# Selective-scan block with a gated FFN: C multiplied in ahead of the transpose, and the sum over states kept in PSUM

## The reference, cut to what matters

```python
h = layernorm(x) * (1 + ca) + sa
dt, B, C = split(h @ x_proj_w.T, [128, 144])          # C: 2048 x 16
delta = softplus(dt @ dt_proj_w.T + dt_proj_b)
for t in tokens:                                       # state s: 256 x 16
    s = exp(delta[t] * A) * s + delta[t] * B[t] * h[t]
    y[t] = sum_n(s[:, n] * C[t, n]) + D * h[t]
x = x + ga * y
h = layernorm(x) * (1 + cb) + sb
x = x + gb * ((silu(h @ gate_w.T * gate_s) * (h @ up_w.T * up_s)) @ down_w.T * down_s)
```

## Time and profile before

| | |
|---|---|
| time, median of 3 (lowest to highest) | 377.23 us (377.08 to 378.97) |
| the profiled execution (span of its trace) | 381.0 us, 3907 instructions |
| first scan starts, last scan ends | 35.2 us, 339.6 us |
| DVE busy from 35.2 to 343 | 95% of it |

### The profile page before, as it was taken

The page is one execution under the profiler, slowest core; times in us unless marked ns, Lnnn a source line. Parts: engine busy times, 40 slices in busy tenths (PEclk is TensorE's granted clock), DMA queues, the critical chain, the costliest instruction groups (busy, mean ns, idle before and its releaser), DMA issues.

```text
span 381.0 us, 3907 instructions
## 1 busy us (share of the span) xinstructions
PE 260.1 (68%) x1212; PEld 197.4 (52%) x1212; DVE 316.1 (83%) x482; ACT 200.0 (52%) x320; POOL 207.9 (55%) x153
## 2 busy tenths in 40 slices
PE   8934544962652679756595897485779756669996
PEld 8534424552541556545374655373557545447774
DVE  2143999799999988999999899999998998993531
ACT  3431644571552686739535868386455556832610
POOL 2007464936597786465768665676685939321000
PEclk9995566775855569968997899779985968699999
DMA  5059940073040500620304216504022700000101
GB/s 171 3 151 369 235 67 0 3 163 60 19 92 1 110 2 0 174 51 20 92 2 73 37 55 137 89 0 112 1 63 48 158 10 0 0 2 0 55 2 58
DMA packets 15958, 25.57 MB, mean 67 GB/s; under 512 B 1344, under 2 KB 6656, under 8 KB 15936
## 3 DMA queue, kind: packets, MB, share of 16 engines
q1 hardware_dynamic: 15520, 24.48, 26.9%
q10 hardware_dynamic: 416, 0.81, 0.6%
HBM read 23.06 MB, written 2.23 MB: 66 GB/s over the span
## 4 chain that ended last, share of the span: by engine, by line
DVE 46%; PE 26%; issue 16%; ACT 6%; DMA 3%; POOL 1%; DVEq 0%; SPq 0%; ACTq 0%; POOLq 0%
DVE state L873 22%; DVE resid L796 11%; PE stateT L1056 5%; PE side L1003 4%; PE side L939 4%; PE side L1036 4%; DMA wmod_sb<-in_wmod 3%; PE side L1020 3%; DVE u L743 2%; DVE gates L771 2%; PE side L916 2%; PE stateT L900 1%; ACT decay L660 1%; DVE resid L708 1%; PE side L953 1%
## 5 line engine op out<-in xcount | busy, mean ns | idle before, releaser
L507 POOL TENSOR_TENSOR state<-u,brow 128x1024 f32<-128x1024 f32 x64 | 152.0, 2384 | 25.1 <-DMA brow<-bT_dram 25.0
L1056 PE MATMUL stateT<-ident,state 128*128 128x128 f32 x512 | 94.2, 336 | 102.1 <-DVE resid L796 68.2
L1056 PEld LDWEIGHTS stateT<-ident,state 128*128 128x128 f32 x512 | 72.7, 172 | 129.9 <-DVE state L873 116.3
L660 ACT ACTIVATE decay<-delta,A 128x512 f32<-128x512 f32 x128 | 87.0, 690 | 87.4 <-DVE state L873 85.0
L873 DVE TENSOR_TENSOR_SCAN state<-decay,last,state 128x512 f32<-128x512 f32 x96 | 117.4, 1264 | 9.2 <-ACT decay L660 9.1
L796 DVE SCALAR_TENSOR_TENSOR resid<-stateT,C_sb,resid 128x256 f32<-128x256 f32 x192 | 78.3, 469 | 0.0
L478 POOL COPY last<-state 128x2 f32<-128x2 f32 x48 | 10.0, 209 | 64.1 <-DVE state L873 63.8
L873 DVE TENSOR_TENSOR_SCAN state<-decay,state 128x512 f32<-128x512 f32 x32 | 37.1, 1202 | 2.8 <-ACT decay L660 2.8
L488 POOL TENSOR_TENSOR acc<-acc,prod 128x1024 f32<-128x1024 f32 x12 | 28.3, 2361 | 17.9 <-ACT prod L642 17.9
L1003 PE MATMUL side<-h_hi,ffn_hi 128*128 128x512 f32 x88 | 34.8, 479 | 0.6 <-DVE gates L771 0.6
L1003 PE MATMUL side<-h_lo,ffn_hi 128*128 128x512 f32 x88 | 30.8, 435 | 2.5 <-POOL h_lo L367 2.5
(11 more groups left out here) (98 smaller groups left out, 302.4 us busy)
## 6 DMA issues: line engine op xcount, KB each, us to landing
brow<-bT_dram SPq DMA_DIRECT2D x16, 1024.0 KB, 8.3
resid<-in_x SPq DMA_DIRECT2D x4, 512.0 KB, 11.1
out<-resid SPq DMA_DIRECT2D x8, 256.0 KB, 2.2
wmod_sb<-in_wmod ACTq DMA_DIRECT2D x1, 768.0 KB, 6.0
wmod_sb<-in_wmod SPq DMA_DIRECT2D x1, 768.0 KB, 11.6
ffn_sb<-in_gateT SPq DMA_DIRECT2D x1, 640.0 KB, 10.3
ffn_sb<-in_upT SPq DMA_DIRECT2D x1, 640.0 KB, 7.8
down_sb<-in_downT SPq DMA_DIRECT2D x1, 640.0 KB, 8.1
```

Of the source, the lines that this page charges most:

```text
L507: nc.gpsimd.tensor_tensor(state[j % RING_STATE][:, :, 0:S], u[:, c % 2, :, 0:S], b.unsqueeze(1).to_broadcast([P, HALVES, S]), ALU.mult).th ...
L660: nc.scalar.activation(decay[i % RING_DECAY][:, 0:S], delta[:, c % 2, h, 0:S], ACT.Exp, scale=A[:, h * N + n:h * N + n + 1]).then_inc(deca ...
L1056: ins = nc.tensor.transpose(to[:, b * D + h * P:b * D + (h + 1) * P], of[:, h, (2 * q + b) * P:(2 * q + b + 1) * P], ident[:, :])
```

## The change

- **C ahead of the transpose.** The scan no longer writes over its input: it reads `drv` (ring of 7) and writes `state` (ring of 4). Then state times C[n] goes back into `drv`, channel-major, in one 128x1024 instruction. DVE does this for states 0, 2, 4, 6, 8, 10, 12, 14, 15 (`times_c`), reading the row of C from the PSUM bank `rows_ps`. PE spreads that row there with a one-hot matmul on C split in two fp32r parts (`spread_row`). POOL does it for states 1, 3, 5, 7, 9, 11, 13 (`keep_c`), with rows of C that a DMA spreads over the partitions (`crow`).
- **Sum in PSUM.** PE's transposes of `drv` carry start=False and accumulate all 16 states, and the D term ahead of them, in the two banks `sums` (`add_state`, `add_dterm`). DVE adds `sums` to `resid` once a chunk (`x2`). `C_sb`, `acc2`, `prod` and the adds of L796 go.
- **Moved to POOL:** cap, u (now delta times `hmodg`, which ACT makes as a second copy of hmod scaled by ga), and nmr. Moved to ACT: the copy to `last`; in step 4 also h2 (from DVE), while lo of chunk 3 moves from DVE to POOL. POOL's drives run three slots ahead (`LEAD`).
- B and C are one product (`bc`), stored and read back together; `chi` (ACT) and `clo` (DVE) split C. Gates are single, and wmod lies in their memory. Side banks are three (six in step 4), placed by table. The tables are rewritten.

```diff
+POOL_C = [1, 3, 5, 7, 9, 11, 13]
+DVE_C = [n for n in range(N) if n not in POOL_C]
+CGROUPS = [POOL_C[:4], POOL_C[4:]]
...
+        (16, "K down0"), (16, "K down1"), (17, "K down2"), (18, "K down3"),
...
-        (6, "F bT"), (6, "B 0"), (7, "S wmod"), (8, "S x"), (10, "S ffn"), (11, "S down"),
+        (6, "F bc"), (6, "B 0"), (6, "C 0"), (7, "S wmod"), (7, "B 1"), (8, "S x"), (10, "S ffn"), (11, "S down"),
...
+AS_TRANSPOSE = True
+LEAD = 3
+ADD_LAG = 2
+KEEP_LAG = 1
...
-RING_STATE = 6
+RING_DRV = 7
+RING_STATE = 4
 RING_B = 2
 GROUP = 4
+RING_C = 2
...
+                first, last = N + at[0], N + at[-1] + 1
+                rows = bc_dram[first:last:2, TOK0[c]:TOK0[c] + CHUNK[c]]
+                sp.dma_start(crow[group % RING_C][:, 0:len(at), 0:CHUNK[c]], rows.partition_broadcast(P))\
+                  .then_inc(crow_loaded[group % RING_C], 16)
...
+                    pool.wait_ge(spexp_ready, HALVES * (c + 1))
+                    nc.gpsimd.tensor_scalar(splus[:, :, 0:S], splus[:, :, 0:S], EXP_CAP, 0.0, ALU.min, ALU.max)\
+                      .then_inc(spcap_ready, 1)
+                elif name == "u":
+
+                    pool.wait_ge(*emptied(("F z", c, HALVES - 1)))
+                    pool.wait_ge(hmod_ready, HALVES * (c + 1))
+                    nc.gpsimd.tensor_tensor(u[:, c % 2, :, 0:S], delta[:, c % 2, :, 0:S], hmodg[:, :, 0:S],
+                                            ALU.mult).then_inc(u_ready, 1)
...
+                if j >= RING_DRV:
+
+                    pool.wait_ge(added, j - RING_DRV + 1)
+                b = brow[(j // GROUP) % RING_B][:, n % GROUP, 0:S]
+                nc.gpsimd.tensor_tensor(drv[j % RING_DRV][:, :, 0:S], u[:, c % 2, :, 0:S],
+                                        b.unsqueeze(1).to_broadcast([P, HALVES, S]),
+                                        ALU.mult).then_inc(drive_ready, 1)
...
+                if m == 0:
+                    pool.wait_ge(crow_loaded[group % RING_C], 16 * (group // RING_C + 1))
                 pool.wait_ge(scan_done, upto_scan(c, n, HALVES - 1))
...
+                row = crow[group % RING_C][:, m, 0:S]
+                nc.gpsimd.tensor_tensor(drv[j % RING_DRV][:, :, 0:S], state[j % RING_STATE][:, :, 0:S],
+                                        row.unsqueeze(1).to_broadcast([P, HALVES, S]),
+                                        ALU.mult).then_inc(prod_pool, 1)
...
+                        for n in range(LEAD):
+                            drive(0, n)
+                    if step >= 0:
+                        for c, n in lagged(step, slot, -LEAD):
+                            drive(c, n)
+                    for c, n in lagged(step, slot, KEEP_LAG):
+                        if n in POOL_C:
+                            keep_c(c, n)
...
+            def keep_last(c, n):
+
+                act.wait_ge(scan_done, upto_scan(c, n, HALVES - 1))
+                nc.scalar.activation(last[:, n, :], state[(c * N + n) % RING_STATE][:, :, CHUNK[c] - 1], ACT.Copy)\
+                  .then_inc(last_kept, 1)
...
+                    dve.wait_ge(added, upto_added(c, N - 1))
                     to = resid[:, BLK0[c]:BLK0[c] + nb, :]
...
+                    nc.vector.tensor_tensor(to, to, sums[:, 0:nb * D].rearrange("p (b d) -> p b d", d=D),
+                                            ALU.add).then_inc(x2_ready, 1)
...
+            def times_c(c, n):
+
+                S, j = CHUNK[c], c * N + n
+                dve.wait_ge(scan_done, upto_scan(c, n, HALVES - 1))
+                dve.wait_ge(row_ready, upto_prod(c, n)[1])
+                nc.vector.tensor_tensor(drv[j % RING_DRV][:, :, 0:S], state[j % RING_STATE][:, :, 0:S],
+                                        rows_ps[:, 0:S].unsqueeze(1).to_broadcast([P, HALVES, S]),
+                                        ALU.mult).then_inc(prod_dve, 1)
...
+            def spread_row(c, n):
+
+                S, count = CHUNK[c], upto_prod(c, n)[1]
+                if n == DVE_C[0]:
+                    pe.wait_ge(*emptied(("F bc", c, 0)))
+                if c == 0 and n == DVE_C[0]:
+                    pe.wait_ge(sel_ready, 1)
+                if count > 1:
+                    pe.wait_ge(prod_dve, count - 1)
+                nc.tensor.matmul(rows_ps[:, 0:S], sel[:, n, :], c_parts[:, c % 2, 0:S],
+                                 start=True, stop=True).then_inc(row_ready, 1)
+
+            def add_dterm(c):
+
+                pe.wait_ge(diag_ready, 1)
+                pe.wait_ge(*emptied(("F xT", c, HALVES - 1)))
+                if c:
+                    pe.wait_ge(x2_ready, c)
+                for b in range(NBLK[c]):
+                    for h in range(HALVES):
+                        ins = nc.tensor.matmul(sums[:, b * D + h * P:b * D + (h + 1) * P],
+                                               hmodg[:, h, b * P:(b + 1) * P], diag_D[:, h, :],
+                                               start=b % 2 == 0 and h == 0, stop=False)
+                ins.then_inc(dterm_done, 1)
+
+            def add_state(c, n):
+
+                j = c * N + n
+                if n == 0:
+                    add_dterm(c)
+                pe.wait_ge(*upto_prod(c, n))
+                of = drv[j % RING_DRV]
+                for b in range(NBLK[c]):
+                    for h in range(HALVES):
+                        ins = nc.tensor.matmul(sums[:, b * D + h * P:b * D + (h + 1) * P],
+                                               of[:, h, b * P:(b + 1) * P], ident[:, :], is_transpose=AS_TRANSPOSE,
+                                               start=False, stop=n == N - 1 and b % 2 == 1 and h == HALVES - 1)
+                ins.then_inc(added, 1)
+
             def run_step(step, full_weights):
...
```

583 lines of the change are left out of this document (271 added, 312 removed), and 20 rows, old and new, of tables (PLACE, PLAN).

## The result

The changed kernel takes 402.38 us (median), the kernel before on the same chip 377.39; the ratio is 1.0595, with a 95% interval of 1.0508 to 1.0682. It is slower by 6%, where I had forecast 360. Its four runs spread widely, from 398.91 to 407.92; the longest was taken while the chip was in a slower state, and the ratio leaves it out. The profiled execution took 400.18 (its span is 398.0); the rest of this document works with spans, 381.0 before and 398.0 after, a difference of 17.0.

The account below looks back on a forecast made before the run. DVE was taken to set the length of a step, PE the tail. From 381.0 us profiled, steps took off 21.6, the start 1.7, the tail added 5.7: 363.4 profiled, 360 predicted as median; range 348 to 380.

Parts of the forecast that it names:

- the start: Step 0 and setup: first scan at 32 us, tokens of chunk 1 at 47, step 1 at 110 against 111.7; 1.7 saved.
- the tail: After the last step's list: add(15) and the norm's chain behind down blocks, gates waiting; 45.8 us instead of 40.1, 5.7 lost.
- ACT's bursts: ACT's work in slots 4 to 6 and slot 9's wait make DVE wait; 4 us a step with F work, bounds 0 and 7.
- the end of the sum at x2: DVE waits at x2 for add(15), behind two blocks of down on PE: 3.4 us in step 2, 3.9 in the last.
- the ledger: Sum of DVE's instruction times in a step, less 0.08 us each: 59.6 us after the change, against 75.6.
- silu, slot 12: Silu and two table loads on ACT stand ahead of the next exp; DVE waits 3.6 us, three times.
- hdn4, slot 15: On DVE, waits for up4, which PE has behind the row for state 15: 1.6 us, three times.
- xT behind x2: xT comes late behind row, dterm, adds and blocks, so ACT's hmod in slot 4 waits about 1.8 us more.
- rival 2: PE falls to half clock where it waits, at x2, xT and the tail's gates: plus 15, about 375 us; chance 0.2.
- Rival 3: POOL becomes the bound, idling through DVE's waits: a step is 77.6 us and the kernel slower, 388; chance 0.14.
- Rival 1: The waits are mostly hidden and steps come to POOL's 64 us, except for x2: about 349 us; chance 0.2.
- Rival 4: The sum in PSUM is no cheaper for PE than its transposes were, and PE is full: about 370 us; chance 0.04.

Follow-up runs that it names:

- the version with the row last: The change with PE issuing the row of C last in each slot, behind the add and the slot's own products: 375.43 us, ratio 0.9879 to the kernel before.
- four mends: The change with down behind the closing add, gate copies a slot after products, chunk 1 tokens first, row last: 363.80 us; with selector and D multiplies later too, 360.52.
- the mended order: The change with down behind the sum, gates spread, tokens first, row last, and selector casts and D multiplies later: 360.52 us, ratio 0.9484 to the kernel before.

## Why the prediction was wrong

The prediction summed three parts: the steps, the start and the tail. Against the 381.0 of before, the span moved by -1.8 at the start, +11.4 in the steps and +7.4 in the tail.

**The steps: -21.6 predicted, +11.4 measured.** This is the step of the prediction that failed, and in it the part "what stands in the way": ACT's bursts, put at 4 us a step, and the end of the sum at x2. Work was priced right: the product at 1.23 (bounds 1.2 and 1.35) took 1196 ns, and the ledger's 58.3 us for step 1 and 59.6 for step 2 are 59.45 and 60.54 in the windows, 1 us more each. The waits, summed from DVE's timeline:

| us, steps 1 / 2 / 3 | predicted | measured |
|---|---|---|
| bursts of ACT | 4 / 4 / 1 | 16.1 / 9.7 / 5.2 |
| of these, slots 3 to 6 | | 5.2 / 1.4 / 0.8 |
| of these, slots 7 to 11 | | 10.9 / 8.4 / 4.4 |
| silu, slot 12 | 3.6 / 3.6 / 3.6 | 3.8 / 3.8 / 3.6 |
| hdn4, slot 15 | 1.6 / 1.6 / 1.6 | 3.4 / 2.0 / 2.0 |
| x2 | none / 3.4 / 3.9 | none / 6.1 / 7.6 |
| xT behind x2 | none / 1.8 / none | in slots 3 to 6 |

- *"Bounds 0 and 7; I take 4 a step."* I summed ACT's own work in slots 4 to 6 against DVE's and took the copies of gates as 0.7 us each. (That sum, at its own rows, is 12.4 us and not 13.) For slots 4 to 6 the size was right. What is missing is slots 7 to 11: in this kernel a copy costs the wait for its product as well, and the exps stand behind the copy. I named a product late on PE for hdn4 ("PE now has behind the row for state 15") and for x2, but not for the five gates. Giving the copies a slot of lead took 13.2 us from DVE's wait for exps, and in slots 7 to 11 it left 6.9 of 23.7; so this leg is shown.

Why the product is late has more than one cause. The row that waits for DVE, as in the turn above, stands directly ahead of the waits in slot 11, 3.9 us in the three steps. In slot 8 of steps 1 and 2 (5.3 us) PE's first gate waits for a side bank that `clo` on DVE has yet to read:

```profile
148.75 0.70 PE L1015 MATMUL side<-h_hi,ffn_hi 128*128 128x512 f32 x2 [2.16 <-DVE c_parts L773]
149.95 0.69 ACT L669 ACTIVATE gates<-side,pack_sb 128x512 f32<-128x512 f32 x1 [3.51 <-PE side L1015]
```

Whether a fourth side bank, as the kernel before has, would remove this wait, no run shows. In slot 9 of the same steps (8.1 us) the third gate has another gate, a row and an add ahead of it; the row and the add wait for nothing, and the clock granted in that stretch was 0.79 and 0.53. This fits the version with the row last, in which slots 7 to 11 still have 20.2 us. With four mends, step 1 has 9.5 us of waits for exps in DVE's timeline, silu included, near the 7.6 predicted.
- *x2.* The chain was right, and each part of it is in the timeline above: product 15, row, add 14, two blocks, add 15. I had its end at 12.1 us into the step; it was 14.6. The difference is PE's clock. Right after the wait of 4.48 the row, the add and the block took 0.76, 1.97 and 3.83, in the version with the row last 0.49 to 0.50, 1.09 and 2.32. That is 2.7 us. The clock that was granted there can be read in windows of the kernel after, around these rows:

```profile
278.90:285.10 6.20, 6.19 (x19) 4.77 (x19) 3.35 (x3) 1.38 (x2) 3.44 (x2) 0.56 0.05 15
285.10:289.80 4.70, 4.70 (x24) 3.47 (x24) 0.00 (x0) 0.00 (x0) 1.21 (x1) 1.00 0.00 0
```

0.56 and then 1.00: first mostly the lower of the two clocks (1.2 GHz), then the full one (2.4). At the start of step 2 it is the same, with the same 4.48 of pause. DVE was at x2 at 8.7 in step 2, as predicted, and at 7.0 in step 3. This is the mechanism of rival 2, at the places where PE had stood still.
- *hdn4* was the right mechanism. It was priced low in step 1.

Of the signs that I had named for being wrong none came: the product took 1.2 us, POOL was busy for 87% of step 1 at most, and the clock was 0.83 in steps 2 and 3. The sign for being right that failed was DVE's idle time, "10 us or so a step": in step 1 it was 23.5.

**The start: 110 predicted, 109.9 measured.** The parts were not all right. The statistics of chunk 1 started at 48.22, after a wait of 11.4 for the tokens (landing predicted for 47). But the first scan started at 34.4 and not at 32. I had missed `sel` and `diag_D` ahead of the first statistics; moving them brought 4.1 us there, in a version whose tokens come first. In the change the 2.4 us don't count, since DVE waits for the tokens right behind that scan. The second scan started at 49.95 (48.9 predicted), and the rest of step 0 took 1.2 us less than I had summed. That the two nearly cancel is luck.

**The tail: +5.7 predicted, +7.4 measured.** The wait for the sum is 6.04 and the gap ahead of the gates is there. PE waits 1.42 for xn, 1.16 for the high part and 2.54 for the low one. In part it came as predicted. Here too the clock was low after the pauses: from 371.0 to 376.5 us it was granted at 0.50, and a pair of gate products took 1.05 us there instead of 0.63. The 7.4 counts from the end of DVE's list, as the prediction did; from the last scan the tail is 51.9 us against 41.4 before. The two versions with four mends show that most of this is order: with the sum closed ahead of the blocks it is 44.3 and 43.9.

**The rivals.** Rival 3 gave the right side and nearly the right size (388), with a wrong mechanism: POOL, the supposed bound, was busy for 65%, and with 30 us less on it the kernel got slower. Its condition, that POOL idles more than 12.4 us a step, was met in steps 2 and 3, but POOL's idle time followed from the waits of the others: taking work from POOL made them longer. Rival 1 (steps of 64, 68 and 64) is what the mended order comes nearest to, with 70.5, 71.9 and 66.0. Of rival 2 there is the clock after a wait: it put 3.4 us more at x2 in steps 2 and 3, and they were 2.7 and 3.7, the second in part because DVE was at x2 earlier; but it had 375 for the whole. Rival 4 has no support: the 512 matmuls that add in PSUM took PE 89.8 us, where the transposes took 94.2, and PE is not full.

Of the whole, 17.0 us, the moves to POOL alone gave -14.2 (366.8 against 381.0), though that was another chip and the difference is good to 2 us or so. What is left for the rest of the change, in the order written, is +31.2. This is a difference of two traces; no run has C ahead of the transpose and the sum in PSUM alone. With the same work in another order the rest is a gain: 0.948 against 0.968 for the moves alone, with intervals that don't meet.

## What to carry to other kernels

When work is moved to an engine that feeds others, list for every waiting instruction what stands behind it in its queue, and who waits for *that*, until the chain comes back to where it began. Here such rings and the late sum made the kernel 17 us longer, though its busiest engine had lost 64 us of work. An instruction that waits for the newest result (here the row, one bank deep) belongs last in its slot, behind everything whose inputs are older; here that gained most at the end of the sum, and little at the exps. A consumer's PSUM copy needs its product a slot ahead, or the consumer's own stream stops with it. A long wait that is removed is a gain only if the next engine in the chain isn't late for another reason: 11.4 us less of waiting for tokens gave 1.8.

## What the hardware showed unexpectedly

- PE accumulates fp32 transposes in PSUM at the pace of plain ones: eight took 1.09 us at the full granted clock, as in the earlier trace rows.
- POOL's cap, one operand of 128x1024, took 1041 ns (I had taken 1.6 us). The Trainium skill, "GPSIMD Engine Reference", in its section on cycle accounting, states 1.03 cycles an element, from which the prediction had an estimate of 0.9 us. The trace is 16% above it, and nearer to it than my 1.6.
